# First mixture: the second batch's gate right behind its turns, in the bank of the turned routing weights, and the third chunk's up products behind the second chunk's down products

## What is computed

```python
scores = sigmoid(x @ gate_W) * route_scale            # x is normalised first
topk_scores, topk_idx = top_k(scores, 2)              # 8 experts
gate_full = the two kept scores over their sum, zero elsewhere
h = gelu(einsum('bsd,edh->bseh', x, W1) + b1)         # 8 experts x 64
y = einsum('bseh,ehd->bsed', h, W2) + b2
out = einsum('bse,bsed->bsd', gate_full, y) + gelu(x @ Ws1 + bs1) @ Ws2 + bs2
```

## Time and profile before

| | us |
|---|---|
| median of 3 runs | 1001.09 |
| lowest, highest | 1000.1, 1003.0 |
| the profiled execution's own time | 1001.73 |
| its span, first to last instruction | 999.6 |
| first mixture in it | about 396 to 463 |

### The profile page before, as it was taken

How to read it: one execution, slowest core, us unless ns; L and a number is a source line. 1 busy time by engine, 2 the same in 40 slices (tenths; PEclk the granted TensorE clock), 3 DMA queues, 4 the chain that set the end, 5 groups by cost and what they waited for, 6 DMA issues and landing times.

```text
span 999.6 us, 16264 instructions
## 1 busy us (share of the span) xinstructions
PE 918.0 (92%) x5620; PEld 534.0 (53%) x5620; DVE 730.8 (73%) x1495; ACT 630.4 (63%) x1263; POOL 360.0 (36%) x401
## 2 busy tenths in 40 slices
PE   3689999999999999977899999999999999998998
PEld 1222232232232233534577777777777776687997
DVE  6899999999999997558645454545454546797877
ACT  3267888888888888335765555555555554465665
POOL 5700000000000011202596848584857472246422
PEclk9789999999999999889999999999999999999999
DMA  3400111110000000000000000000000011000000
GB/s 69 159 29 24 39 39 50 34 42 25 22 18 24 10 1 12 1 1 7 1 1 11 1 6 12 1 1 6 11 1 1 6 49 37 1 1 11 12 11 12
DMA packets 23370, 20.03 MB, mean 20 GB/s; under 512 B 5176, under 2 KB 17440, under 8 KB 23288
## 3 DMA queue, kind: packets, MB, share of 16 engines
q1 hardware_dynamic: 23288, 18.99, 6.4%
HBM read 14.26 MB, written 4.59 MB: 19 GB/s over the span
## 4 chain that ended last, share of the span: by engine, by line
PE 67%; DVE 21%; issue 4%; ACT 3%; POOL 2%; DMA 2%; SPq 1%; DVEq 0%; ACTq 0%; POOLq 0%
DVE halves L814 13%; PE a_sum L2129 10%; PE summed L1028 7%; PE m_down L2393 6%; PE a_turn L2120 5%; PE score_bank L1015 5%; PE max_bank L975 4%; PE a_scores L1662 3%; PE a_scores L1663 3%; PE a_scores L1664 3%; PE max_bank L988 3%; PE a_proj L2139 3%; PE m_hid L2213 1%; DVE a_lowest L1672 1%; PE m_hid L2214 1%
## 5 line engine op out<-in xcount | busy, mean ns | idle before, releaser
L939 ACT ACTIVATE probs<-score_bank 128x512 f32<-128x512 f32 x512 | 267.6, 601 | 74.4 <-PE score_bank L1015 74.2
L814 DVE TENSOR_REDUCE halves<-max_bank 128x2 f32<-128x1024 f32 x256 | 298.7, 1219 | 11.0 <-PE max_bank L975 8.9
L1677 ACT ACTIVATE a_probs<-a_scores,a_lowest 128x896 f32<-128x896 f32 (+7 forms) x128 | 94.9, 742 | 108.3 <-DVE a_lowest L1672 107.7
L2129 PE MATMUL a_sum<-a_turned,a_v 128*128 128x512 f32 (+3 forms) x384 | 158.6, 500 | 1.4 <-ACT a_headsT L2026 1.3
L975 PE MATMUL max_bank<-k_stack,q_stack 48*128 48x512 bf16 x512 | 117.7, 397 | 24.8 <-DVE halves L814 24.5
L1028 PE MATMUL summed<-probs,v_tile 128*32 128x512 f32 x1024 | 137.2, 608 | 0.0
L1015 PE MATMUL score_bank<-q_stack,k_stack 50*128 50x512 bf16 x512 | 132.1, 384 | 4.6 <-ACT probs L939 2.2
L1672 DVE TENSOR_REDUCE a_lowest<-a_scores 128x1 f32<-128x896 f32 (+7 forms) x128 | 96.2, 755 | 35.0 <-PE a_scores L1666 34.5
L737 POOL COPY v_tile<-values 128x128 f32<-128x128 f32 x16 | 4.7, 295 | 303.5 <-PE summed L1028 303.3
L2120 PE MATMUL a_turn<-identity,a_probs 128*128 128x128 f32 x576 | 95.2, 274 | 5.4 <-ACT a_probs L1677 4.4
L1921 DVE COPY a_turned<-a_turn 128x512 f32<-128x512 f32 x96 | 57.4, 598 | 52.0 <-PE a_turn L2120 51.7
(11 more groups left out here) (315 smaller groups left out, 1644.3 us busy)
## 6 DMA issues: line engine op xcount, KB each, us to landing
rope<-in_rope SPq DMA_DIRECT2D x8, 256.0 KB, 3.0
rope<-in_L_ffn_mlp_w SPq DMA_DIRECT2D x8, 256.0 KB, 4.6
q_parts<-l_q_parts SPq DMA_DIRECT2D x2, 768.0 KB, 4.9
k_parts<-l_k_parts SPq DMA_DIRECT2D x2, 768.0 KB, 6.5
q_stack<-q_parts SPq DMA_DIRECT2D x30, 48.0 KB
k_stack<-k_parts SPq DMA_DIRECT2D x30, 48.0 KB
x<-in_L_attn_x SPq DMA_DIRECT2D x2, 512.0 KB, 4.1
q_stack<-shift SPq DMA_DIRECT2D x64, 2.0 KB
```

What stands on the lines that cost most here:

```text
L814: dve.reduce_max(halves[:, u % 2, half, :].rearrange("p (x t) -> p x t", x=2)[:, :, qt], max_bank[place % RING][:, :, :], AX_X).then_inc(f ...
L939: act.activation(probs[:, step % PROBS, x, :], score_bank[e % SCORES][:, :], ACT.Exp, scale=SCALE0).then_inc(prob_ready, 1)
L1677: act.activation(probs[:, k % 2, c, 0:row_width(n)], scores[n % 2][:, 0:row_width(n)], ACT.Exp, bias=lowest[:, n % 8:n % 8 + 1], accum_out ...
L2129: pe.matmul(sum_bank[:, skipped(k, j):CH], v[:, BLOCKS[k][0], j, :], turned[:, m % SLOTS, skipped(k, j):CH], start=(j == 0), stop=(TURNED_ ...
```

## The change

The gate's results get the right half of the bank whose left half holds the turned routing weights (`m0_routing`). The gate's first half stands right behind the turns of chunk 3, the second behind the shared expert's down product of chunk 1. The up products of chunk 2 stand behind down products of chunk 1 instead of ahead of its spreads and between all of its steps; the last three of them stand in a row behind the last down product. ACT makes the exponential before it touches chunk 2, and takes chunk 1's sum out behind the third Gelu of chunk 2 instead of the fifth. DVE weighs three pairs of chunk 1 before it ranks, and the fourth before it marks. POOL copies the weights of chunk 1 before it splits chunk 2.

```diff
-        part_bank = ps("m0_part", [3 * E0, CH], BF16)
+        routing_bank = ps("m0_routing", [P, CH])
+        part_bank, gate_bank = routing_bank[0:3 * E0, 0:CH // 2].bitcast(BF16), routing_bank[:, CH // 2:CH // 2 + TB * E0]
...
             take_parts(1)
-            weigh_hidden(1, 0)
-            weigh_hidden(1, 1)
+            for m in range(3):
+                weigh_hidden(1, m)
             dve.wait_ge(prob_ready, 1)
             m0.rank(dve, chain, 1)
-            weigh_hidden(1, 2)
+            weigh_hidden(1, 3)
             m0.mark(dve, chain, 1)
-            weigh_hidden(1, 3)
             m0.weigh(dve, chain, 1).then_inc(parts_ready, 1)
...
                 pool.wait_ge(part32_ready, c + 1)
-                if c < FIRST:
-                    pool.wait_ge(tr_out, c + 1)
-                    m0.raise_in(pool, FIRST + c).then_inc(tr_high, 1)
-                    pool.wait_ge(tr_high, c + 1)
-                    m0.lower_in(pool, FIRST + c).then_inc(tr_low, 1)
-                    pool.wait_ge(tr_low, c + 1)
                 if c == 1:
+                    split_turned(0)
+                    split_turned(1)
...
             take_turned(FIRST + 1)
+            act.wait_ge(gate_ready, 2)
+            m0.score(act, gate_bank, 1).then_inc(prob_ready, 1)
             for j in range(3):
                 activate(act, 2, j)
-            act.wait_ge(gate_ready, 2)
-            m0.score(act, spare, 1).then_inc(prob_ready, 1)
+            leave(1)
             for j in range(3, NU):
                 activate(act, 2, j)
-            leave(1)
...
+            def gate(part):
+                pe.wait_ge(tr_out, part + 1)
+                if part == 0:
+                    pe.wait_ge(partT_out, FIRST)
+                m0.gate(pe, gate_bank, 1, part).then_inc(gate_ready, 1)
...
+            turn_in(FIRST + 1)
+            gate(0)
+
+            first_weights(1)
+            sum_shared(1)
+            gate(1)
+            sum_expert(1, 0)
+            spread_weights(1, 2)
+            pe.wait_ge(done.freed, done.last_place + 1)
+            turn_sum(0)
+            sum_expert(1, 1)
+            spread_weights(1, 3)
+            up(pe, 2, 0)
+            sum_expert(1, 2)
+            up(pe, 2, 1)
+            sum_expert(1, 3)
+            for j in range(2, NU):
+                up(pe, 2, j)
+            pe.wait_ge(parts_ready, 1)
+            turn_parts(2)
+            up(pe, 3, 0)
```

More of the change, by code:

```diff
@@ L1233, in take_parts @@
                 dve.wait_ge(partT_ready, c + 1)
-                dve.tensor_copy(weightT[:, cols], part_bank[:, :]).then_inc(partT_out, 1)
+                dve.tensor_copy(weightT[:, cols], part_bank).then_inc(partT_out, 1)
             def weigh_hidden(c, m):
@@ L1300, in on_gpsimd, with split_turned @@
         def on_gpsimd(pool):
+            def split_turned(c):
+                pool.wait_ge(tr_out, c + 1)
+                m0.raise_in(pool, FIRST + c).then_inc(tr_high, 1)
+                pool.wait_ge(tr_high, c + 1)
+                m0.lower_in(pool, FIRST + c).then_inc(tr_low, 1)
+                pool.wait_ge(tr_low, c + 1)
             for c in range(NCH):
@@ L1364, in turn_parts @@
                 for k in range(4):
-                    last = pe.transpose(part_bank[:, k * P:(k + 1) * P],
-                                        m0.parts[:, 4 * c + k, :, :].rearrange("p a e -> p (a e)"), m0.identity16[:, :])
+                    last = pe.transpose(part_bank[:, k * P:(k + 1) * P], m0.parts[:, 4 * c + k, :, :].rearrange("p a e -> p (a e)"), m0.identity16[:, :])
                 last.then_inc(partT_ready, 1)
@@ L1384, in turn_next, with sum_shared, sum_expert, first_weights @@
                 transpose_tiles(pe, hid_bank[c], a1.normed, t.identity[:, :], c).then_inc(next_turned, 1)
+            def gate(part):
[3 more added lines that the diff above has]
+                m0.gate(pe, gate_bank, 1, part).then_inc(gate_ready, 1)
+            def sum_shared(c):
+                wait_from(pe, out_ready, c)
+                pe.wait_ge(act_ready, c * NU + 1)
+                pe.wait_ge(part32_ready, c + 1)
+                pe.matmul(sum_bank[:, :], m0.ws2[:, :], shared[m0.shared_rows, c % 2, :], start=True, stop=False).then_inc(shared_used, 1)
+            def sum_expert(c, m):
+                pe.wait_ge(weighed_ready, c * NP0 + (m + 1))
+                last = pe.matmul(sum_bank[:, :], m0.w2[:, m, :], weighed[:, m, :], start=False, stop=(m == NP0 - 1))
+                if m == NP0 - 1:
+                    last.then_inc(sum_ready, 1)
+            def first_weights(c):
+                pe.wait_ge(partT_out, c + 1)
+                spread_weights(c, 0)
+                spread_weights(c, 1)
             pe.wait_ge(done.mix_weighed, 1)
@@ L1389, in on_tensor @@
             up(pe, 0, 3)
[L1390 to L1400, removed]
+            first_weights(0)
+            up(pe, 0, 4)
+            up(pe, 1, 0)
+            sum_shared(0)
+            sum_expert(0, 0)
+            spread_weights(0, 2)
+            up(pe, 1, 1)
+            sum_expert(0, 1)
+            spread_weights(0, 3)
+            up(pe, 1, 2)
+            turn_parts(1)
+            sum_expert(0, 2)
+            up(pe, 1, 3)
+            turn_in(FIRST)
+            sum_expert(0, 3)
+            up(pe, 1, 4)
+            turn_in(FIRST + 1)
[18 more added lines that the diff above has]
+            up(pe, 3, 0)
+            for c in range(FIRST, NCH):
+                first_weights(c)
+                sum_shared(c)
                 for m in range(NP0):
[L1402 to L1405, removed]
+                    sum_expert(c, m)
                     if m + 2 < NP0:
@@ L1409, in on_tensor @@
                         up(pe, c + 1, m + 1)
[L1410 to L1423, removed]
+                    if m == 0:
                         turn_sum(c - 1)
[L1425 to L1428, removed]
+                    if c == FIRST and m == 0:
                         turn_parts(3)
-                    if c + 2 < NCH and m == NP0 - 1:
-                        up(pe, c + 2, 0)
                     if c == NCH - 1 and m in (1, 2):
```

## The result

The changed kernel takes 993.22 us in the median of its runs (991.35 to 996.87), the kernel before 1001.09; the ratio is 0.9926, with a 95% interval of 0.9905 to 0.9947. That is 7.9 us, or 0.74%, less. 991.9 was forecast, with a range of 987.0 to 996.5.

What follows compares the result with a forecast made beforehand. TensorE, busy 92% of the span, was taken as the bound, losing time to idle spots and low clock. 12.3 us less 3.1 for a clock fall leaves 9.2; 1001.73 less 9.2, less 0.64 to the median, gives 991.9, range 987.0 to 996.5.

Steps and rivals of the forecast that it cites:

- The two waits go: First mixture: TensorE's waits of 1.4 us for POOL's split and 4.6 us for DVE were to vanish.
- 12.3 us sooner at full clock: Chunk 2's spreads on TensorE at 427.4 instead of 439.75, without any wait and at full clock.
- the 13.73 us of the sum: TensorE's work from 413.7 to chunk 2's spreads: gates, spreads, down and up products, turned sum and parts, at full-clock prices.
- POOL costs nothing: POOL's split for chunk 2 ends at 414.9, about 0.2 us later, before `up(2, 0)` at 420.3.
- ACT and DVE: Scores by 418.8; DVE's 6.3 us chain from 419.3 ends at 425.6, hidden by 0.7 us before the turned parts at 426.3.
- The clock: In the mixture: one fall to low clock taken as likelier, 6.8 us long, losing 3.1 us and leaving 9.2; chance 0.51.
- the prediction's own list of signs: Wrong if TensorE waits at turned parts or a Gelu, low stretch absent or over 10.2 us, or end not sooner.
- The rival without a fall: Gates and spreads pass at full clock in the mixture: the whole 12.3 us, so 988.8; chance 0.20.
- the 3.1 us taken off for a fall in the mixture: Loss from 6.8 us of low clock at 0.46 per microsecond, subtracted from 12.3 to leave 9.2.
- The saving is carried to the end: Behind chunk 2's spreads the order is unchanged, so their gain reaches the end; rival, saving waited away, chance 0.05.

Runs made afterwards that it cites:

- the kernels that wait 0.56 or 1.83 us: 0.56: changed kernel with chunk 2's up products and POOL's splits in old places, 992.39 us; 1.83: changed kernel, TensorE awaiting POOL's split before the gate, 997.29 us.
- its other profile: The kernel before, run again unchanged for a second profile: 997.8 us, interval from chunk 3's turns to chunk 2's spreads 21.09 us.
- the wait put back: Changed kernel with TensorE waiting for POOL's first split before the first gate half: 997.29 us, ratio 0.9963 to the kernel before.
- the kernel without the wait for POOL: Kernel before with chunk 2's first up product behind chunk 1's first pair's down product and POOL's order as in the changed kernel: 1001.48 us.
- the kernel with the late gate: Changed kernel with both gate halves back among chunk 1's steps, up products and POOL's order kept: 994.48 us.
- the last kernel: Changed kernel with ACT's chunk 2 sum before chunk 3's last Gelu and DVE's two chunk 2 weighings before the statistics: 992.97 us, again 990.43.

## Why the prediction was right, and where it wasn't

*The two waits go.* Right, to the tenth: 1.4 and 4.6 us are gone, and no new one of size came.

*12.3 us sooner at full clock.* Right in size: the spreads came 12.65 us sooner and the interval shrank by 12.9, since the 13.73 us of the sum were 13.16 in fact. The gate was mis-sized: from its start to the next product a half took 0.89 and 0.81, where the 0.99 was a shown length from the chain, not a distance from start to start. And the first half began at 413.77, 0.17 us ahead of the shown end of the turns.

*POOL costs nothing.* Right: the first split ended at 415.70, 0.8 us later than before (0.6 counted from the turns) and not 0.2, and its product began at 420.08.

*ACT and DVE.* The table load was put behind the gate and the load back behind the first up product; both run ahead of these and are hidden. The chain's end was forecast at 425.6 and came at 425.7, because the third weighing, not the exponential, held the ranking back, as computed. The cover was forecast as 0.7 us and is 0.25, since TensorE was at the turned parts at 425.95 and not at 426.3.

*The clock.* This step failed, and by the prediction's own list of signs: the stretch at 0.50 is absent from the mixture. "I take a fall as likelier", 6.8 us long, stood against six profiles of seven without a fall there (the changed kernel twice and four of its variants), and one with 3.4 us; with the gate in this place, 6.8 us came only in the kernels that wait 0.56 or 1.83 us close to it. The rival without a fall was the true one in the mixture. That the total still came within 1.3 us of the forecast is luck: the 3.1 us taken off for a fall in the mixture were not lost there but, as far as the profiles tell, on two other accounts. One is the reference: the profile of before, against which the 12.3 us were reckoned, had 17 us of low clock in this place, more than its other profile, where the interval was 21.1. Against that one the change is worth 7.3 us: the two waits, 5.9, and 3.4 us of low clock, 1.4. Against the first it is 12.9: 5.9 and 17.1 x 0.41 = 7.0. The other is that the changed kernel's executions have low stretches too, at other places: 1.5 us of the profile's gain went at 854.8, and the profiled execution was the shortest of its five, 1.9 us under their median. How much of the 7.9 us between the medians is the clock's is therefore known only roughly: 5.9 are the waits, about 2 remain.

*The saving is carried to the end.* Right but for that: 12.0 us were left ahead of 854.8 and 10.5 at the end.

The Trainium skill, page "TensorE: Matmul & The Clock Gate", section "HAM oscillation — how this bites in real kernels", which lays the low clock to idle gaps, is borne out by the wait put back, by the falls around all waits of 3.5 and 4.6 us, and by the 13.76 us at full clock. It is not the whole: the 3.4 us at 417.3 followed no gap, and no fall followed the gap of 1.36 us in the second profile of before. The section "What's actually happening" of that page says that the monitor runs freely and isn't started by a kernel; that agrees with equal code at unequal clocks here.

Open: what lengthened seven executions of the kernel without the wait for POOL to 1001 to 1005 us, since the one profile is of a shorter one; and why moving the weighing alone met 13.7 us of low clock. Whether the two groups differ in the mixture would take profiles of executions above 1001 us.

## What to carry to other kernels

A latency chain through three engines (a small product, an exponential, a ranking) can be hidden behind wide work of the engine that waits for it. Whether that work stands between or behind the other steps mattered little here, as long as there was enough of it behind the small product and the exponential didn't stand behind work of its own engine. Either part of the change alone gave nearly all, with ACT's new order in both, so try the parts before the whole. Count an idle spot of TensorE by its length and then by the clock behind it, but over several executions: one profile of before would have promised 12.9 us, another 7.3, and the medians gave 7.9.

## What the hardware showed that I had not expected

ACT's table load did not wait for the product that its activation reads: it started at 414.73, 2.4 us before the exponential, and in the kernel with the late gate 5.6 us before (418.56 and 424.21). So the two loads of the changed kernel, 1.28 us each, cost nothing. It isn't always so: in the kernel before the load back to Gelu did wait,

```profile
433.07 1.28 ACT L1201 ACT_TABLE_LOAD   x1 [3.12 <-DVE m_weighed L1240]
```

3.1 us behind the exponential, until DVE's weighing was over (432.31 + 0.69). What makes a load wait is open: this one stands ahead of a Gelu that needs DVE's weighing and TensorE's product, the hidden ones ahead of activations that need TensorE's work only. The Trainium skill, page "ScalarE: Activation LUTs", section "What ACT_TABLE_LOAD costs", gives 1283 ns for a load and 1380 ns of drain for each switch; the load is 1.28 us here too, but no drain shows behind it, in the kernel before the exponential began 0.01 us after the load's end (428.44 + 1.28, 429.73).

A microsecond of low clock cost 0.41 to 0.48 us of time in this mixture (the two profiles of before and the last kernel 0.41, the wait put back 0.48), a little less than the half that the clock alone would make. The same program's executions on one chip differ by up to 7.9 us (the changed kernel, 989.1 to 996.97), and the longer ones mostly have the lower mean clock.
